# Two-layer decoder, last cross attention: two heads per instruction, score products on four row groups, and the outputs of 16 heads summed in one PSUM tile

## The chip, the core and the metric

One core of a Trainium2 chip runs one program. The metric is the device time of one execution in microseconds. The engines are TensorE (PE; its weight loads are listed as PEld), VectorE (DVE), ScalarE (ACT), GpSimd (POOL) and SyncE (SP), which issues most DMAs. They run side by side and are held in order by semaphores only.

## What is computed

Four sequences of 256 tokens with 128 channels go through two decoder layers. Only the end of layer 1 is touched by the change: its cross attention over a context of 256 tokens, followed by a mixture of experts. With 16 heads of 8 channels each, and `x` of one sequence (256 x 128), the last attention is

```
q = x @ Wq + bq;  k = ctx @ Wk + bk;  v = ctx @ Wv + bv      # each 256 x 128, 16 heads of 8
a[h] = softmax(q[h] @ k[h].T * 8 ** -0.5, axis=keys)         # 256 x 256 for each head
o[:, 8h:8h+8] = a[h] @ v[h]
x = layernorm(x + o @ Wo + bo)                               # then 8 experts, 2 of them per token
```

Everything is fp32. For the scores, q and k are split into a high and a low part, which are stacked along the contraction (3 x 8 rows for one head, 24 of a group of 32), and run as fp32r products.

## The kernel before

The five engines walk through one list of slots (`through_slots`), from slot -14 to slot 345. In a slot, each engine does its `front`, then what is due of the side jobs (`sides`: projections, the output projection and norms, the experts), then its `back`. There is no other scheduler: the order on each engine is the order of this walk. The last attention has one head per slot, from slot `LX_AT` = 235 on. Slots are counted from there in this text ("slot 10" is 235 + 10). Heads are numbered through all attentions; here n is 0 to 63 for the 4 sequences of 16 heads, four heads make a unit, four units a sequence (the code calls it a batch).

For head n, in slots:

- n: PE `head_products` multiplies queries by keys (two matmuls with 31 rows of contraction, lines 721 to 744) into the PSUM tile `SC[0]`, half n % 2; DVE `head_maximum` (L1542) takes the maximum over the 256 keys, 128x512 elements. PE may write a half again once the maximum of head n - 2 is done.
- unit start + 6 (`TURN_AT`): PE turns the maxima of the unit (`turn_shifts`, L750), ACT copies them to `shift_rows` (L1135), and SP sends them with one DMA into row 31 of each group of `packed_q` (`place_shifts`, L1804).
- n + 9 (`SHIFT_LAG`): PE `transposed_products` (L769, two matmuls, 32 rows) writes scores minus maximum, keys on partitions, into `SC[1]`, half n % 2; ACT `head_exponential` (L1169) takes the exponential, 128x512, into one of 8 buffers `exps`.
- n + 10: POOL `add_key_tiles` (L1689) adds the two key tiles of the head, 128x256, into `kept` (a part of the tile VB).
- unit start + 15 (`SUMS_AT`): PE `unit_sum` (L786) sums `kept` over keys with a matrix of ones, the unit's four heads on four column groups.
- unit start + 16 and 17: ACT copies the sums and takes exp(-ln(sum)) as a first inverse (L1162, L1163, L1175), POOL checks it (L1701), DVE refines it (L1559).
- unit start + 17 (`VALUES_AT`): PE `unit_values` (L812) multiplies values by exponentials, four heads on four column groups, into `SO`. A head has 8 channels but fills 32 rows of its group.
- unit start + 18 (`DIVIDE_AT`): DVE `divide` (L1567) writes the unit's 128x256 normalised outputs to `OB`. So there are four such tiles for a sequence.

`mix(b)` is the side job of sequence b after its last unit, from slot 16 b + 31 on (`OUT_AFTER` = 31): `project_out` (L625) at its steps 1 and 2 multiplies four 128-row chunks of `OB` by a padded Wo, for each of two token tiles; then come the norm, the router (L909, L915 to L917), and at steps 15 to 28 the experts (L923, L938, L948, L958, L969) and the last norm. The mixes of two sequences overlap with each other and with the heads of later sequences; slot 110 is the last.

Rows of a matmul decide its row group: head n sits on partitions 32 (n % 4) to 32 (n % 4) + 31 of `packed_q` and `packed_k`. In a slot the order on PE is: products of head n (front), turn, side jobs, sums and values, products of head n - 9 (back), then the products of head n + 1 in the next front.

SP's list in these slots: `place_shifts` every fourth slot, six small DMAs for each unit of the next sequences at slots 14 to 42 (`cross_in`, L1821), and the loads of the experts (`load_experts`, L1809, two of 512 KB each) at slots 8, 12, 16 and 20.

## Time and profile before

| | |
|---|---|
| time, median of 3 runs | 796.15 us (793.91 to 796.48) |
| the profiled execution | 796.1 us, of which the span in the trace is 794.3 us |
| PE busy | 719.1 us (91%), 5852 matmuls |
| PE weight loads busy | 542.2 us (68%) |
| DVE busy | 489.1 us (62%) |
| ACT busy | 412.9 us (52%) |
| POOL busy | 290.0 us (37%) |
| mean granted TensorE clock | 0.937 of full |
| first products of the last attention | 592.8 us |
| last products of the last attention | 737.4 us |

Times in the rows count from the span's start. An engine's busy time counts the instructions in flight; matmuls overlap, so a busy PE is not yet a PE at its peak. The granted clock is the share of TensorE's full 2.4 GHz: 1.00 is 2.4 GHz, 0.50 is 1.2 GHz, and a value between is a mean over a stretch with both.

### The profile page before, as it was taken

What the parts mean: (1) busy time and instruction counts of PE and PEld (TensorE: products, weight loads), DVE (VectorE), ACT (ScalarE), POOL (GpSimd) and SP (SyncE); (2) the same over time, 40 slices, a digit from 0 to 9 for tenths busy, and PEclk for the clock granted to TensorE, in tenths of its full rate; (3) what the DMA queues carried; (4) which work ended last, traced back from release to release, by engine and by line L of the source; (5) the groups of instructions that cost most, each with busy time, mean ns of one, the idle gap of its engine ahead of it and who ended that gap; (6) DMA issues with size and microseconds to landing.
All of it is one profiled execution on the core that took longest, in us unless ns stands there. A gap on an engine that the chain in (4) does not pass through costs nothing.

```text
span 794.3 us, 16402 instructions
## 1 busy us (share of the span) xinstructions
PE 719.1 (91%) x5852; PEld 542.2 (68%) x5852; DVE 489.1 (62%) x1297; ACT 412.9 (52%) x1047; POOL 290.0 (37%) x395
## 2 busy tenths in 40 slices
PE   8788889898897998999999989989888899999886
PEld 6565567575665765899898967758566455767665
DVE  4669777887977885444543455545455658583643
ACT  2234556657566677554544467555562545454311
POOL 0015355565555666110000036423350646363300
PEclk8869989999999999999999999999998756999999
DMA  8537451533727471000000000001011501000000
GB/s 235 126 69 179 123 128 43 122 83 88 161 46 205 112 214 57 2 1 1 1 1 1 1 1 4 1 2 41 4 38 54 185 26 31 2 2 9 8 7 7
DMA packets 25175, 48.11 MB, mean 61 GB/s; under 512 B 7264, under 2 KB 14192, under 8 KB 25096
## 3 DMA queue, kind: packets, MB, share of 16 engines
q1 hardware_dynamic: 24376, 45.66, 22.7%
q10 hardware_dynamic: 720, 1.41, 0.5%
q8 instruction: 48, 0.79, 0.4%
q14 instruction: 31, 0.25, 0.1%
HBM read 17.49 MB, written 0.52 MB: 23 GB/s over the span
## 4 chain that ended last, share of the span: by engine, by line
PE 60%; DVE 14%; issue 10%; ACT 8%; SPq 3%; POOL 2%; DMA 2%; POOLq 0%; ACTq 0%; DVEq 0%
PE SC L839 7%; PE G L550 7%; PE SC L826 7%; PE SC L769 5%; PE G L625 4%; PE SC L861 3%; PE G L938 3%; DVE shift_cols L1542 3%; PE SO L812 3%; ACT causal_probs L1154 2%; PE SO L893 2%; PE SC L743 2%; PE G L647 2%; SPq L1769 1%; PE G L577 1%
## 5 line engine op out<-in xcount | busy, mean ns | idle before, releaser
L1169 ACT ACTIVATE exps<-SC 128x512 f32<-128x512 f32 x192 | 114.4, 597 | 106.8 <-PE SC L769 106.1
L1542 DVE TENSOR_REDUCE shift_cols<-SC 128x2 f32<-128x512 f32 x192 | 129.5, 684 | 32.0 <-PE SC L743 31.5
L1621 POOL TENSOR_TENSOR rstd<-variance,consts 128x2 f32<-128x2 f32 (+1 forms) x48 | 36.8, 766 | 266.0 <-DVE variance L1234 263.0
L1689 POOL TENSOR_TENSOR VB<-exps 128x256 f32<-128x256 f32 x128 | 95.7, 756 | 59.4 <-ACT exps L1169 58.6
L1143 ACT ACTIVATE hidden<-SC,cols 128x256 f32<-128x256 f32 x128 | 53.6, 471 | 65.4 <-PE SC L826 65.3
L1711 POOL TENSOR_TENSOR causal_probs<-causal_probs,inverse 128x256 f32<-128x256 f32 x64 | 51.6, 828 | 68.9 <-DVE inverse L1555 68.9
L1576 DVE SCALAR_TENSOR_TENSOR R<-SC,small,R 128x128 f32<-128x128 f32 x128 | 39.0, 346 | 54.0 <-PE SC L839 53.3
L1154 ACT ACTIVATE causal_probs<-SC,negmax 128x128 f32<-128x128 f32 (+1 forms) x128 | 52.3, 424 | 37.1 <-DVE negmax L1550 37.0
L769 PE MATMUL SC<-stacked_q,stacked_k 100*128 100x256 f32 x256 | 66.9, 344 | 3.5 <-DMA stacked_q<-shift_rows 1.9
L839 PEld LDWEIGHTS SC<-ffn_w,hidden 128*128 128x128 f32 x512 | 66.0, 192 | 5.3 <-issue 1.8
L839 PE MATMUL SC<-ffn_w,hidden 128*128 128x128 f32 x512 | 67.6, 276 | 0.0
L826 PE MATMUL SC<-XN,ffn_w 128*128 128x256 f32 x256 | 66.5, 383 | 0.0
L1681 POOL TENSOR_TENSOR VB<-exps,consts 128x256 f32<-128x256 f32 x64 | 46.6, 739 | 44.8 <-ACT exps L1169 44.7
L769 PEld LDWEIGHTS SC<-stacked_q,stacked_k 100*128 100x128 f32 x256 | 40.3, 193 | 32.9 <-issue 21.9
L743 PE MATMUL SC<-stacked_k,stacked_q 96*128 96x256 f32 x256 | 56.5, 305 | 6.3 <-DVE shift_cols L1542 5.9
L1550 DVE TENSOR_REDUCE negmax<-SC 128x2 f32<-128x256 f32 x64 | 32.7, 553 | 41.2 <-PE SC L864 41.2
L1701 POOL TENSOR_TENSOR unit_sums<-unit_sums,unit_inverse 128x256 f32<-128x256 f32 x48 | 35.7, 744 | 60.8 <-ACT unit_inverse L1175 60.8
L550 PE MATMUL G<-XN,a_weights 128*128 128x256 f32 x184 | 49.2, 410 | 2.4 <-DVE Z L1320 1.5
L743 PEld LDWEIGHTS SC<-stacked_k,stacked_q 96*128 96x128 f32 x256 | 41.7, 200 | 10.8 <-DVE shift_cols L1542 9.4
L826 PEld LDWEIGHTS SC<-XN,ffn_w 128*128 128x128 f32 x256 | 44.2, 192 | 4.2 <-issue 0.8
L812 PE MATMUL SO<-exps,VB 128*32 128x256 f32 (+1 forms) x640 | 46.4, 404 | 0.0
L550 PEld LDWEIGHTS G<-XN,a_weights 128*128 128x128 f32 x184 | 35.9, 205 | 8.8 <-DVE Z L1320 1.8
(257 smaller groups left out, 1504.5 us busy)
## 6 DMA issues: line engine op xcount, KB each, us to landing
stacked_k<-k_hi SPq DMA_DIRECT2D x64, 128.0 KB, 2.4
stacked_q<-q_hi SPq DMA_DIRECT2D x64, 128.0 KB, 2.4
ffn_w<-in_ffn_w SPq DMA_DIRECT2D x16, 512.0 KB, 4.8
stacked_k<-k_lo SPq DMA_DIRECT2D x32, 128.0 KB, 2.4
stacked_q<-q_lo SPq DMA_DIRECT2D x32, 128.0 KB, 2.5
packed_k<-U SPq DMA_DIRECT2D x48, 32.0 KB, 1.9
packed_q<-YN SPq DMA_DIRECT2D x48, 32.0 KB, 1.9
a_weights<-in_a_li SPq DMA_DIRECT2D x3, 256.0 KB, 7.4
```

What stands on the lines that cost most here:

```text
L550: last = mm(g[:, k * T:(k + 1) * T], w[kr, c * P:(c + 1) * P], src[kr, :], start=True, stop=True)
L743: last = mm(SC[0][:, n % 2, t, :], q[:, t * P:(t + 1) * P], kk, start=True, stop=True)
L769: last = mm(SC[1][:, n % 2, t, :], kk[:, t * P:(t + 1) * P], q, start=True, stop=True)
L812: last = mm(g[HD * k:HD * k + HD, q0:q0 + w], v, src, start=first, stop=end)
L826: last = mm(g[:, f * T:(f + 1) * T], experts0[e // 4][0][:, at:at + P], XN[b][:, :], start=True, stop=True)
L839: last = mm(g[:, t * C:(t + 1) * C], hidden0[i % 4][:, f, t * P:(t + 1) * P], experts0[e // 4][1][:, at:at + C], start=f == 0, stop=f == 1)
L1143: last = fn(hidden0[i % 4][:, f, :], g[:, f * T:(f + 1) * T], ACT.Gelu, bias=col("ffn0_b1", 2 * e + f))
L1154: last = fn(PB[:, i % RING, k, 0:w], SC[i % 2][:, j, t, 0:w], ACT.Exp, bias=negmax[:, i % 4, k:k + 1], accum_out=sums[:, i % 4, k:k + 1])
L1169: fn(exps[:, n % EXPS, :, :].rearrange("p t q -> p (t q)"), SC[1][:, n % 2, :, :].rearrange("p t q -> p (t q)"), ACT.Exp, scale=ATTENTIONS ...
L1542: v.tensor_reduce(shift_cols[:, n // UNIT % 4, :, n % UNIT], SC[0][:, n % 2, :, :], axis=AX.X, op=ALU.max, negate=True).then_inc(head_max, 1)
L1689: v.tensor_tensor(kept[n % EXPS].rearrange("p t q -> p (t q)"), exps[:, n % EXPS, 0, :], exps[:, n % EXPS, 1, :], ALU.add).then_inc(kept_r ...
L1711: last = v.tensor_tensor(p, p, m, ALU.mult)
```

## The change

- Scores: PE works in even slots only. One block (`cross_products`) holds the products of heads n and n + 1 and the transposed ones of heads m and m + 1, with m = n - 10 (`CROSS_LAG` = 10 where it was 9), in the order n, n + 1, m, m + 1 for the first tile and then for the second: four row groups and four PSUM banks. It waits until the maxima of heads n - 2 and n - 1, and the exponentials of heads m - 2 and m - 1, are done.
- DVE (`two_maxima`), ACT (`two_exponentials`, now in `front`) and POOL (`add_key_tiles_of_two`) do two heads with one instruction.
- The value tile is spread: 32 columns for each head, zero but for its 8 channels at the place of its unit, so that the four units of a sequence add up in one 128x256 tile of `SO`. Their sums over keys do the same in the other half of `SO`, with a new constant `own_rows`. POOL clears the two value tiles once (`clear_values`); DVE writes the values in two strided instructions.
- Inverse, check, refinement and division are done once per sequence instead of once per unit, after its last values.
- `project_out` multiplies one chunk instead of four. The mix of each sequence starts one slot later (`CROSS_OUT_AFTER` = 32).

```diff
-SHIFT_LAG = 9
+SHIFT_LAG, CROSS_LAG = 9, 10
+CROSS_INVERT, CROSS_REFINE, CROSS_DIVIDE = 18, 19, 19
+CROSS_OUT_AFTER = HEADS - UNIT + CROSS_DIVIDE + 1
...
-    "lx": {"lx_wq": (C, C), "lx_wo": (P, 512)},
+    "lx": {"lx_wq": (C, C), "lx_wo": (C, C)},
...
 def project_out(s, t):
-                    if at["d"] == HD:
+                    if s // NB == LX:
+                        c0, chunks = 4 * (s % 2), 1
+                        pe.wait_ge(cross_divided, CROSS_UNIT + s % NB + 1)
+                    elif at["d"] == HD:
...
+                def cross_products(n, m):
+                    if n is not None:
...
+                        pe.wait_ge(head_max, n)
+                        if n % UNIT == 0:
+                            pe.wait_ge(packed_in[n // UNIT % 4], 16 * 6 * (stream_of(n) % NB + 1))
+                    if m is not None:
+                        pe.wait_ge(head_exp, m)
+                        if m % UNIT == 0:
+                            pe.wait_ge(shifts_in[m // UNIT % 4], 16 * (m // UNIT // 4 + 1))
+                    for t in range(TT):
+                        of = slice(t * P, (t + 1) * P)
+                        if n is not None:
+                            for h in (n, n + 1):
+                                q, kk = packed(h, HD - 1)
+                                last = mm(SC[0][:, h % 2, t, :], q[:, of], kk, start=True, stop=True)
...
+                        if m is not None:
+                            for h in (m, m + 1):
+                                q, kk = packed(h, HD)
+                                last = mm(SC[1][:, h % 2, t, :], kk[:, of], q, start=True, stop=True)
...
+                def cross_sum(U_):
+                    n, u = UNIT * U_, U_ % 4
+                    if u == 0:
+                        cross_place(stream_of(n) % NB)
+                    pe.wait_ge(kept_ready, n + UNIT)
+                    own = const("own_rows")[:, HD0 * (3 - u):HD0 * (3 - u) + HD]
+                    for k in range(UNIT):
+                        mm(SO[HD * k:HD * k + HD, T:2 * T], own, kept[(n + k) % EXPS].rearrange("p t q -> p (t q)"),
+                           start=u == 0, stop=False)
...
+                def cross_unit_values(U_):
...
+                    pe.wait_ge(head_exp, n + UNIT)
+                    for kt in range(TT):
+                        for k in range(UNIT):
+                            last = mm(SO[HD * k:HD * k + HD, 0:T], cross_value(s, kt, h0 + k), exps[:, (n + k) % EXPS, kt, :],
+                                      start=False, stop=u == 3 and kt == TT - 1)
+                    last.then_inc(cross_outputs, 1)
...
+                def cross_sums_drawn(b):
...
+                    act.wait_ge(cross_outputs, CROSS_UNIT + 4 * (b + 1))
+                    fn(unit_sums[:, b % 2, :], SO[:, T:2 * T], ACT.Copy)
+                    fn(unit_inverse[:, b % 2, :], SO[:, T:2 * T], ACT.Ln).then_inc(cross_drawn, 1)
...
+                def two_exponentials(n):
+                    unit_read(act, (n - EXPS) // UNIT)
+                    act.wait_ge(head_scores, n + 2)
+                    fn(exps[:, n % EXPS:n % EXPS + 2, :, :].rearrange("p h t q -> p (h t q)"),
+                       SC[1][:, :, :, :].rearrange("p h t q -> p (h t q)"), ACT.Exp, scale=ATTENTIONS[LX]["scale"]).then_inc(head_exp, 2)
...
+                def two_maxima(n):
+                    dve.wait_ge(shift_scores, n + 2)
+                    v.tensor_reduce(shift_cols[:, n // UNIT % 4, :, n % UNIT:n % UNIT + 2].rearrange("p t h -> p h t"), SC[0][:, :, :, :],
+                                    axis=AX.X, op=ALU.max, negate=True).then_inc(head_max, 2)
...
+                def cross_refine(b):
+                    dve.wait_ge(inverse_checked, CROSS_UNIT + b + 1)
+                    v.scalar_tensor_tensor(unit_inverse[:, b % 2, :], unit_sums[:, b % 2, :], -2.0,
+                                           unit_inverse[:, b % 2, :], op0=ALU.add, op1=ALU.mult)\
+                        .then_inc(sums_inverse, 1)
+
+                def cross_divide(b):
+                    dve.wait_ge(cross_outputs, CROSS_UNIT + 4 * (b + 1))
+                    dve.wait_ge(sums_inverse, CROSS_UNIT + b + 1)
+                    v.scalar_tensor_tensor(OB[:, 4 * (b % 2), :], SO[:, 0:T], -1.0, unit_inverse[:, b % 2, :],
+                                           op0=ALU.mult, op1=ALU.mult).then_inc(cross_divided, 1)
...
+                    k = n % EXPS
+                    both = VB[k // 4][:, 1024 + T * (k % 4):1024 + T * (k % 4 + 2)].rearrange("p (h q) -> p h q", q=T)
+                    v.tensor_tensor(both, exps[:, k:k + 2, 0, :], exps[:, k:k + 2, 1, :], ALU.add).then_inc(kept_ready, 2)
...
+                def clear_values(k):
+
+                    wait_filled(pool, ("OC", 4 * (NB - 2 + k) + 3))
+                    v.memset(VB[k][:, 0:TT * HEADS * HD], 0.0).then_inc(packed_cleared, 1)
```

## Rows read from the trace of the kernel before

**Rows 1.** Windows by stage: span, busy time of each engine (instructions), granted clock, DMA share, GB/s.
```profile
592.00:612.50 20.50, 17.47 (x128) 13.16 (x128) 10.25 (x25) 6.46 (x14) 3.05 (x4) 0.90 0.13 44
612.50:648.70 36.20, 32.71 (x221) 16.10 (x220) 21.65 (x36) 19.28 (x45) 19.28 (x27) 0.64 0.36 118
648.70:674.10 25.40, 24.39 (x186) 14.36 (x185) 20.40 (x50) 12.66 (x32) 14.96 (x20) 0.70 0.12 30
674.10:711.20 37.10, 36.13 (x358) 25.89 (x357) 25.81 (x71) 18.33 (x42) 16.48 (x23) 0.97 0.01 2
711.20:743.70 32.50, 31.41 (x308) 23.18 (x306) 17.84 (x57) 14.96 (x34) 14.88 (x21) 1.00 0.02 6
743.70:794.30 50.60, 38.95 (x340) 31.82 (x340) 22.41 (x71) 8.78 (x16) 3.83 (x5) 0.95 0.03 9
```

**Rows 2.** The same windows, only instructions on packed_q: PE, PEld, POOL busy, clock, DMA.
```profile
612.50:648.70 36.20, 15.51 (x92) 10.03 (x92) 0.00 (x0) 0.64 0.36 118
648.70:674.10 25.40, 9.30 (x58) 5.86 (x56) 0.00 (x0) 0.70 0.12 30
674.10:711.20 37.10, 8.07 (x64) 4.79 (x64) 0.00 (x0) 0.97 0.01 2
711.20:743.70 32.50, 5.49 (x24) 3.23 (x24) 0.00 (x0) 1.00 0.02 6
...
sum 202.30, PE 42.65 PEld 26.45 POOL 0.00; mean PE 7.11 PEld 4.41 POOL 0.00
```

**Rows 3.** PE timeline, one block between side jobs: start us, duration, line, operation, tiles.
```profile
688.82 0.38 PE L769 MATMUL SC<-packed_q,packed_k 32*128 32x256 f32 x1
...
689.26 2.00 PE L938 MATMUL G<-slot_tokens,ffn_w 128*128 128x64 f32 x16
```

**Rows 4.** PE timeline at 708 us: two slots' products with nothing between them.
```profile
707.95 0.38 PE L769 MATMUL SC<-packed_q,packed_k 32*128 32x256 f32 x1
707.96 0.38 PE L743 MATMUL SC<-packed_k,packed_q 31*128 31x256 f32 x1
707.97 0.38 PE L769 MATMUL SC<-packed_q,packed_k 32*128 32x256 f32 x1
707.97 0.38 PE L743 MATMUL SC<-packed_k,packed_q 31*128 31x256 f32 x1
...
708.40 1.07 PE L812 MATMUL SO<-exps,VB 128*32 128x256 f32 x16
```

**Rows 5.** Groups of instructions by line and shape, 600 to 794 us: count, busy, mean ns, idle.
```profile
L1689 POOL TENSOR_TENSOR VB<-exps 128x256 f32<-128x256 f32 x64 | 48.7, 769 | 39.5 <-ACT exps L1169 39.1
L1542 DVE TENSOR_REDUCE shift_cols<-SC 128x2 f32<-128x512 f32 x61 | 41.1, 685 | 11.4 <-PE SC L743 11.3
L1169 ACT ACTIVATE exps<-SC 128x512 f32<-128x512 f32 x64 | 38.1, 599 | 36.1 <-PE SC L769 35.6
...
L1701 POOL TENSOR_TENSOR unit_sums<-unit_sums,unit_inverse 128x256 f32<-128x256 f32 x16 | 12.2, 764 | 19.9 <-ACT unit_inverse L1175 19.9
...
L625 PE MATMUL G<-w_lx_wo,OB 128*128 128x128 f32 x64 | 10.4, 312 | 0.4 <-DVE HE L1525 0.4
...
L1162 ACT ACTIVATE unit_sums<-SM 128x256 f32<-128x256 f32 x16 | 6.1, 380 | 3.6 <-PE SM L786 3.6
```

**Rows 6.** Group of the whole span: DVE maximum over half as many elements.
```profile
L1550 DVE TENSOR_REDUCE negmax<-SC 128x2 f32<-128x256 f32 x32 | 13.6, 425 | 41.2 <-PE SC L864 41.2
```

**Rows 7.** SP's queue, timeline from 625 us: issue of shifts and of the next sequence's parts.
```profile
625.88 0.55 SPq L1804 DMA_DIRECT2D packed_q<-shift_rows  x1
626.52 1.76 SPq L1821 DMA_DIRECT2D packed_k<-U  x3
...
631.34 0.55 SPq L1804 DMA_DIRECT2D packed_q<-shift_rows  x1
```

**Rows 8.** PE timeline, the longest wait for shifts.
```profile
635.70 0.57 PE L769 MATMUL SC<-packed_q,packed_k 32*128 32x256 f32 x1 [1.52 <-DMA packed_q<-shift_rows]
```

**Rows 9.** A window of 2 us, columns as in rows 1.
```profile
642.00:644.00 2.00, 2.00 (x20) 0.81 (x19) 0.00 (x0) 0.84 (x3) 0.00 (x0) 0.50 0.07 17
```

210 lines of the change are left out of this document (143 added, 67 removed).

## Prediction

> **What bounds the kernel now.** I read the windows by stage first [rows 1]. The last attention runs from 592 us to the end, and I cut it where its side jobs change: stage A (slots 0 to 9, beside the rest of the attention before it), B (slots 10 to 33, nearly only heads, with the expert weights coming in), C (slots 33 to 46, the first sequence's norm and router), D (47 to 62, with experts of one sequence), E (63 to 78), F (the rest, no heads after slot 72). PE is busy for 36.1 of 37.1 us in D and for 31.4 of 32.5 us in E, at a clock of 0.97 and 1.00. So D and E are as long as PE's list is. In B and C PE is busy too (32.7 of 36.2, 24.4 of 25.4), but at 0.64 and 0.70: much of the list runs at 1.2 GHz, as in the window at 642 us, which has no idle time and a clock of 0.50 [rows 9]. In C, DVE is busy for 20.4 of 25.4 us and is a close second. In F PE is busy for 39 of 50.6 us, and the chain through the experts of the last sequence sets the time.
>
> Then I read what the products cost in each stage [rows 2]: 42.65 us in all, and by difference 4.3 us in A. Then what one block costs: a head's transposed products and the next head's plain ones, four matmuls on two row groups, hold PE from 688.82 to 689.26, 0.44 us [rows 3]. And where no side job stands between two slots, eight matmuls on four row groups start within 0.02 us of each other in fours, and the next job starts 0.45 us after the first [rows 4]. That is the change's block, already in the trace: eight for the price of four.
>
> **Products, PE.** After the change there are 32 even slots with a pair n and 32 with a pair m, ten slots behind: 27 blocks hold both and 5 + 5 hold one, 37 in all, of two waves each. In flight a block takes about 0.50 us at 2.4 GHz (0.44 and the tail of the last matmul), and at a clock of 0.65 to 0.70 about 0.65. A: 5 blocks, 2.5 us instead of 4.3. B: 12, 7.8 instead of 15.5. C: 7, 4.6 instead of 9.3. D: 8, 4.0 instead of 8.1. E: 5, 2.5 instead of 5.5 [rows 2]. PE saves 1.8 + 7.7 + 4.7 + 4.1 + 3.0 = 21.3 us.
>
> By the Trainium skill, page "TensorE: Matmul & The Clock Gate", section "Measured speedup vs the span model", four row tiles gave 3.07 times and not 4 times one. By that a full block would take 0.44 x 4 / 3.07 = 0.57 us and the forecast below would be 27 x 0.13 = 3.5 us later. The trace's 0.45 us for eight [rows 4] does not agree with it, and I go by the trace.
>
> **Output projection, PE.** 64 instructions and 10.4 us become 16 and 2.6 us [rows 5], saving 7.8: about 2.8 in C, where the clock is lower, and 1.6 to 1.7 in D, E and F each. Sums, values and turns keep their count and form, only with another stationary tile and other PSUM columns. So PE's list gets 29 us shorter. That is the most that can arrive.
>
> **DVE, ACT, POOL.** DVE's maximum costs 0.685 us for 512 elements and 0.425 for 256, so 1.02 ns for an element more: 1.21 us for two heads instead of 1.37 [rows 5, 6]. ACT: 0.60 for 512, 0.38 for 256, so 1.04 us instead of 1.20 [rows 5]. POOL's add of two heads lies between 0.77 and twice that [rows 5]; nothing on PE needs it before two slots later, so it is covered. Twelve of the sixteen inversions and divisions go: on POOL 12 x 0.76 = 9 us [rows 5], on DVE some 1.1 us for each, on ACT about 1.2. None of these engines is the bound outside C. The spread values cost DVE about 0.2 us for each of four sequences, POOL's two clears (1024 elements) about 1 us each in its idle time. The wider constants add 28 KB at the start: 0 to 0.3 us, I take 0.2.
>
> **The new waits.** (1) One block waits for maxima and exponentials of the pair before, and there is no second half to write into. Its round is the block, 0.5, DVE's 1.21 and two handovers, about 1.9 us for two slots. Now two slots take 3.1 us in B (36.2 / 23 slots x 2) and more elsewhere, so it is covered unless DVE comes to its maxima 1.2 us late. Queued behind PE's wait are the side jobs of both slots. (2) ACT's exponential moves from back to front, past the side jobs, and ahead of the shift copy in every second even slot; the shifts leave up to 1.04 us later and are needed one slot later. (3) SP's list is the same. With expert loads a unit takes it 5.46 us (625.88 to 631.34), without them 0.55 + 2 x 1.8, about 4.2 [rows 7]. This is a floor for B that the change leaves: B moves 5.75 units, three of them with loads, 3 x 5.4 + 2.75 x 4.2 = 28 us. To that come the wait for shifts behind the loads (1.5 us now [rows 8]) and, at slot 28, the next sequence's parts, whose tiles are free only when SP's six DMAs have landed, some 2.5 us. So B ends near 32. (4) The division comes once, after the last values of a sequence: three ACT steps of 0.4, POOL's 0.76, two DVE steps of at most 0.7 and the handovers, 3.5 us in a row [rows 5]. Between those values (slot 77 for the last sequence) and its projection (slot 81) PE has three full slots of the experts of the sequence before, 2.0 us and more each (32.5 us / 16 slots in E [rows 1]). Covered; if the cover were gone it would cost up to 3.5 us, once.
>
> **What arrives.** A: its pace is set by the older attention's softmax; 1.2 of 1.8. B: 36.2 to about 31.7, 4.5 of 7.7. C: PE's list falls to 24.4 - 4.7 - 2.8 = 16.9 us, DVE's to 20.4 - 1.1 - 2.4 = 16.9; neither packs without gaps, so about 20, saving 5.5. D: 4.1 + 1.6 = 5.7, of which 5.0, since joint waits cost a little. E: 4.6, of which 4.0. F: 1.6, of which 1.2. Sum 1.2 + 4.5 + 5.5 + 5.0 + 4.0 + 1.2 = 21.4, less 0.2 for the start: 21.2 us. The profiled execution took 796.1 us (span 794.3 and 1.8 around it), 0.05 from the median, so no correction: 796.1 - 21.2 = 774.9, say 775.
>
> **The rivals.** *The light stages keep their length* (0.16). In A to C, SP's list, the way of the shifts (maxima, turn, exponential, copy, DMA) and DVE take the place of PE, and only D, E, F arrive: 10 us, 786. For it speaks [rows 7], and that DVE is at 20.4 of 25.4 in C; against it, that PE has no idle time at 642 us at 1.2 GHz [rows 9], so that its list is the bound just there. The Trainium skill, page "TensorEngine Tiling (Array Packing)", section "PSUM Bottleneck", says that after a fourfold faster TensorE the PSUM copies may become the bottleneck; that would be this case, with the 1.9 us round as its pace.
>
> *All of PE's gain arrives* (0.16). 29 us, 767. Against: the SP floor in B. For: with four groups in a block TensorE does as much in less time; if the granted clock in B and C rises over 0.64 and 0.70, the gain there is larger than I counted, down to 763.
>
> *The four groups run one after the other* (0.05), so that the change does not do what it says: a block of eight costs 0.88, the products save nothing, and the projection and the fewer small steps leave 7 us: 789. [Rows 4] speaks against.
>
> *The clock falls in D and E* (0.04). PE less busy between joint waits could be granted 1.2 GHz for a part of it; 57 us of its list lie there after the change, and a third of it at half clock costs 19 us: 794. Against: those stages stay dense with expert matmuls, and keep 0.97 and 1.00 now with 1 us of idle time each.
>
> *One buffer is too few* (0.06), the slower side. If DVE, in order, reaches the maxima of a pair only after its side jobs, each of the 23 pairs of A to C exposes its 1.21 us and handovers, 1.4 x 23 = 32 us, against 14 us saved on PE's list there and 10 in D to F: 796 + 32 - 24 = 804. It decides once the round is longer than the 3.1 us that two slots take now.
>
> The forecast keeps 0.53, with 769 to 782 as its own range. The range that should hold 8 in 10 takes in the full gain and most of the light-stage case: 764 to 788. About 0.3%, or 2.4 us, is what a measurement can tell from no change: slower 0.06, same 0.04 (the clock case), faster 0.90.
>
> **What would show it.** The page of the changed kernel should have the same 256 product matmuls in 37 blocks of up to eight, with fours starting within 0.03 us; 16 projection instructions; DVE's maximum x32 near 1.21 us and ACT's exponential x32 near 1.04. The time from first to last products should fall from 144.5 us to about 126, D's 16 slots from 37 to about 32. The forecast is wrong if PE shows waits on the maxima or exponentials of more than 5 us in all, if waits for shifts grow over 5 us, or if a full block takes over 0.6 us at full clock.

## The result, and the profile after

The changed kernel took 800.89 us (median of 20 runs, 796.26 to 813.3) beside 794.97 us of the kernel before; the ratio is 1.0076, 95% interval 1.0054 to 1.0099. Taken again with other runs of both it was 1.0061 (1.0019 to 1.0103). So it is slower by 0.6 to 0.8%, some 6 us, where 21 us less was forecast. Medians hold all runs of a kernel, while the ratios here and below leave out its disturbed, slower runs.

The profiled execution has a span of 804.4 us. Windows by stage, which answer [rows 1]; the markers are the same jobs, the stages A to E up to the last product block at 742.3 us, then everything behind it. Columns: span, then busy time and instructions of PE, PEld, DVE, ACT and POOL, granted clock, DMA share, GB/s.

```profile
598.20:618.40 20.20, 15.98 (x128) 12.15 (x128) 10.48 (x20) 5.88 (x11) 3.21 (x4) 0.92 0.16 53
618.40:655.80 37.40, 24.94 (x217) 11.21 (x217) 17.49 (x20) 16.31 (x25) 15.70 (x14) 0.69 0.35 110
655.80:681.10 25.30, 20.02 (x181) 10.60 (x182) 18.90 (x38) 7.63 (x12) 9.39 (x8) 0.70 0.10 28
681.10:716.00 34.90, 31.61 (x346) 22.09 (x345) 24.73 (x58) 15.26 (x25) 12.60 (x12) 0.96 0.01 2
...
598.20:742.30 144.10, 115.12 (x1078) 72.39 (x1080) 85.29 (x162) 55.75 (x90) 50.65 (x45) 0.83 0.14 43
742.30:804.40 62.10, 48.48 (x410) 38.69 (x409) 27.08 (x92) 10.88 (x20) 6.22 (x7) 0.88 0.02 7
```

The kernel before, from its first to its last products and behind them, in the same columns:

```profile
592.80:737.40 144.60, 136.65 (x1132) 88.96 (x1132) 90.37 (x213) 68.88 (x157) 65.24 (x87) 0.83 0.14 43
737.40:794.30 56.90, 44.41 (x404) 35.56 (x403) 27.71 (x93) 10.80 (x22) 6.50 (x9) 0.95 0.03 8
```

That pair of lines is the case in short. From the first to the last products PE does 21.5 us less (136.65 to 115.12), and the stretch is as long as before (144.6 and 144.1): PE now waits. And the part behind the last products, in which the change only takes work away, takes 5.2 us more, at a clock of 0.88 instead of 0.95.

There may be a third part, ahead of the first products, where little but the constants and weights loaded at the start differs. The first products come at 598.2 instead of 592.8 us. In the five profiles of kernels without the tile for 16 heads, the experiments below included, they come at 588.4 to 593.7, in the mean 591.3. In the fifteen with it they come at 589.7 to 600.1, in the mean 595.0, although the time at a clock of 0.50 ahead of them is nearly the same (46 and 47 us). Most of the difference is there by 300 us already. It is larger than the scatter within the two groups leads one to expect (2 and 3 us from profile to profile), and no experiment looked for its cause. What follows is about the other two parts.

Each engine's work became what was forecast. PE's instructions on the score tiles (whole stage, compare [rows 2], 42.65 us):

```profile
sum 206.20, PE 22.55 PEld 13.95 POOL 0.00; mean PE 3.76 PEld 2.33 POOL 0.00
```

PE's timeline, one full block; the next job starts 0.44 us after the first product, where [rows 4] had 0.45:

```profile
695.37 0.38 PE L796 MATMUL SC<-packed_k,packed_q 31*128 31x256 f32 x2
695.38 0.39 PE L802 MATMUL SC<-packed_q,packed_k 32*128 32x256 f32 x2
695.60 0.28 PE L796 MATMUL SC<-packed_k,packed_q 31*128 31x256 f32 x2
695.60 0.28 PE L802 MATMUL SC<-packed_q,packed_k 32*128 32x256 f32 x2
695.81 0.37 PE L755 MATMUL G<-w_ctx_wk,CTXT 64*128 64x128 f32 x1
```

Groups from 600 us on (compare [rows 5]): busy time and mean ns behind the bar, then idle time ahead of them.

```profile
L1858 POOL TENSOR_TENSOR VB<-exps 128x512 f32<-128x512 f32 x32 | 41.4, 1295 | 44.8 <-ACT exps L1290 24.9 <-issue 19.9
L1680 DVE TENSOR_REDUCE shift_cols<-SC 128x4 f32<-128x1024 f32 x32 | 39.1, 1222 | 24.2 <-PE SC L796 24.2
L1290 ACT ACTIVATE exps<-SC 128x1024 f32<-128x1024 f32 x32 | 32.8, 1024 | 48.5 <-PE SC L802 48.4
...
L1710 DVE SCALAR_TENSOR_TENSOR unit_inverse<-unit_sums,unit_inverse 128x256 f32<-128x256 f32 x4 | 4.9, 1222 | 1.9 <-POOL unit_sums L1874 1.9
...
L662 PE MATMUL G<-w_lx_wo,OB 128*128 128x128 f32 x16 | 4.0, 332 | 5.6 <-DVE HE L1658 3.5 <-issue 2.1
```

PE's waits between first and last products: total, times, longest. First the kernel before, then the changed one.

```profile
PE SC L743 <- DVE shift_cols L1542: 3.0, 5, 1.4
...
PE SC L769 <- DMA packed_q<-shift_rows: 1.5, 1, 1.5
```

```profile
PE SC L796 <- DVE shift_cols L1680: 9.2, 8, 2.8
PE G L503 <- DVE X L1372: 5.8, 2, 3.2
PE SC L796 <- DMA packed_q<-shift_rows: 4.3, 2, 3.3
PE G L662 <- DVE HE L1658: 3.1, 2, 2.4
PE SC L796 <- ACT causal_probs L1249: 2.1, 1, 2.1
PE G L662 <- issue: 2.1, 1, 2.1
```

The maxima (L1680) and the norm of a sequence (L1372), both DVE's, lead. In all PE is idle for 29.0 us of the stretch, where it was idle for 8.0. One way in which DVE comes late shows at 663 us. DVE's timeline, POOL's, and PE's; in brackets the idle time and what ended it:

```profile
663.07 2.50 DVE L1372 TENSOR_SCALAR X<-R,moments,rstd 128x128 f32<-128x128 f32 x2 [0.82 <-POOL rstd L1778]
665.50 1.22 DVE L1680 TENSOR_REDUCE shift_cols<-SC 128x4 f32<-128x1024 f32 x1
```

```profile
663.01 2.48 POOL L1858 TENSOR_TENSOR VB<-exps 128x512 f32<-128x512 f32 x2
```

```profile
665.63 0.44 PE L503 MATMUL G<-consts,X 128*128 128x128 f32 x2 [3.19 <-DVE X L1372]
```

Two norm instructions between SBUF tiles take 2.50 us and end within 0.1 us of POOL's two long additions; PE waits 3.19 us for the norm, and the maxima come last. The kernel before has this meeting too: the same norm took 1.62 us beside two additions of 0.73 us, and those of the next two sequences, which met none, 0.59 us. DVE's timeline of the kernel before:

```profile
655.29 1.62 DVE L1244 TENSOR_SCALAR X<-R,moments,rstd 128x128 f32<-128x128 f32 x2
```

A like meeting lies in the division of three of the four sequences (a refinement takes 1.47 to 1.51 us there). POOL's timeline, then DVE's and PE's:

```profile
652.88 0.73 POOL L1874 TENSOR_TENSOR unit_sums<-unit_sums,unit_inverse 128x256 f32<-128x256 f32 x1 [5.33 <-ACT unit_inverse L1271]
653.57 1.27 POOL L1858 TENSOR_TENSOR VB<-exps 128x512 f32<-128x512 f32 x1
```

```profile
653.64 1.47 DVE L1710 SCALAR_TENSOR_TENSOR unit_inverse<-unit_sums,unit_inverse 128x256 f32<-128x256 f32 x1 [0.86 <-POOL unit_sums L1874]
```

```profile
655.75 0.76 PE L662 MATMUL G<-w_lx_wo,OB 128*128 128x128 f32 x2 [2.12 <-issue]
```

PE's 2.12 us ahead of the projection ("issue" in the profile, but the projection needs the division, which DVE does at 655.23) are the end of that chain.

### The profile page after: what moved, and what is told of

Same layout as the page of the kernel before. It is cut to its first block, busy times and chain, and to the rows that moved or that the text cites. A ratio compares the mean times of both kernels' runs of the same rounds, so it can differ in the third digit from the quotient of the medians.

```text
span 804.4 us, 16062 instructions
## 1 busy us (share of the span) xinstructions
PE 706.1 (88%) x5804; PEld 532.1 (66%) x5804; DVE 483.6 (60%) x1245; ACT 399.9 (50%) x979; POOL 276.9 (34%) x353
## 3 DMA queue, kind: packets, MB, share of 16 engines
q10 hardware_dynamic: 720, 1.44, 0.5%
## 4 chain that ended last, share of the span: by engine, by line
PE 58%; DVE 18%; issue 11%; ACT 7%; DMA 2%; POOL 2%; SPq 2%; POOLq 0%; ACTq 0%; DVEq 0%
PE G L584 7%; PE SC L923 7%; PE SC L910 7%; PE G L662 3%; PE SC L945 3%; PE SC L825 3%; PE G L1022 3%; DVE shift_cols L1675 3%; ACT causal_probs L1249 2%; PE SO L977 2%; PE SO L895 2%; PE SC L770 2%; DVE shift_cols L1680 2%; PE G L684 2%; PE G L1042 2%
## 5 line engine op out<-in xcount | busy, mean ns | idle before, releaser
L1284 ACT ACTIVATE exps<-SC 128x512 f32<-128x512 f32 x128 | 76.3, 597 | 76.5 <-PE SC L825 76.3
L1675 DVE TENSOR_REDUCE shift_cols<-SC 128x2 f32<-128x512 f32 x128 | 86.5, 683 | 19.3 <-PE SC L770 18.9
L1726 DVE SCALAR_TENSOR_TENSOR R<-SC,small,R 128x128 f32<-128x128 f32 x128 | 39.0, 346 | 54.0 <-PE SC L923 53.3
L1290 ACT ACTIVATE exps<-SC 128x1024 f32<-128x1024 f32 x32 | 32.8, 1024 | 48.5 <-PE SC L802 48.4
L1858 POOL TENSOR_TENSOR VB<-exps 128x512 f32<-128x512 f32 x32 | 41.4, 1295 | 44.8 <-ACT exps L1290 24.9
L1844 POOL TENSOR_TENSOR VB<-exps 128x256 f32<-128x256 f32 x64 | 47.6, 753 | 21.4 <-ACT exps L1284 21.1
L1680 DVE TENSOR_REDUCE shift_cols<-SC 128x4 f32<-128x1024 f32 x32 | 39.1, 1222 | 24.2 <-PE SC L796 24.2
L584 PE MATMUL G<-XN,a_weights 128*128 128x256 f32 x184 | 50.6, 419 | 2.6 <-DVE Z L1448 1.5
```

The lines of the kernel that those rows point to most:

```text
L584: last = mm(g[:, k * T:(k + 1) * T], w[kr, c * P:(c + 1) * P], src[kr, :], start=True, stop=True)
L1284: fn(exps[:, n % EXPS, :, :].rearrange("p t q -> p (t q)"), SC[1][:, n % 2, :, :].rearrange("p t q -> p (t q)"), ACT.Exp).then_inc(head_ex ...
L1675: v.tensor_reduce(shift_cols[:, n // UNIT % 4, :, n % UNIT], SC[0][:, n % 2, :, :], axis=AX.X, op=ALU.max, negate=True).then_inc(head_max, 1)
L1680: v.tensor_reduce(shift_cols[:, n // UNIT % 4, :, n % UNIT:n % UNIT + 2].rearrange("p t h -> p h t"), SC[0][:, :, :, :], axis=AX.X, op=ALU ...
L1844: v.tensor_tensor(kept[n % EXPS].rearrange("p t q -> p (t q)"), exps[:, n % EXPS, 0, :], exps[:, n % EXPS, 1, :], ALU.add).then_inc(kept_r ...
```

## The experiments

Theory 1: the joint waits of a pair hold PE. Theory 2: DVE's queue is held, by the division once per sequence and by POOL's long additions. Theory 3: the granted clock takes part of the time. Theory 4: the shifts' DMAs come late, behind expert loads. The table has every kernel that was run; "ratio" is against the kernel before in the same rounds, the rest is from each kernel's one profile: length from first to last products and behind them, and in brackets the us of it at a clock of 0.50.

| kernel | median, us | ratio (95%) | first to last | behind |
|---|---|---|---|---|
| before | 794.97 | 1 | 144.5 (48) | 56.9 (5) |
| before_again | 794.97 | one run | 146.1 (51) | 56.9 (5) |
| changed | 800.89 | 1.0076 (1.0054 to 1.0099) | 144.2 (48) | 62.1 (15) |
| changed_again | 800.02 | 1.0061 (1.0019 to 1.0103) | 145.3 (58) | 60.5 (11) |
| pair_only | 801.04 | 1.0088 (1.0056 to 1.0119) | 144.0 (41) | 57.1 (1) |
| pair_adds | 794.37 | 1.0007 (0.9974 to 1.0040) | 140.2 (38) | 58.1 (6) |
| pair_adds_loads | 798.15 | 1.0051 (1.0022 to 1.0080) | 144.6 (58) | 61.7 (15) |
| tile_only | 796.18 | 1.0013 (0.9989 to 1.0037) | 139.7 (48) | 71.0 (38) |
| tile_loads | 800.56 | 1.0101 (1.0028 to 1.0174) | 140.5 (44) | 61.6 (14) |
| no_refine | 796.07 | 0.9987 (0.9948 to 1.0025) | 141.2 (51) | 59.6 (8) |
| single_adds | 797.55 | 1.0010 (0.9977 to 1.0043) | 136.4 (38) | 65.8 (26) |
| adds_loads | 796.48 | 1.0042 (1.0012 to 1.0073) | 135.8 (38) | 62.1 (15) |
| adds_loads_divide | 796.69 | 0.9994 (0.9959 to 1.0028) | 138.3 (48) | 72.8 (42) |
| split_waits | 797.30 | 1.0030 (1.0000 to 1.0061) | 138.9 (48) | 62.1 (15) |
| half_maxima | 794.70 | 0.9934 (0.9898 to 0.9969) | 136.5 (51) | 63.7 (19) |
| short_adds | 791.62 | 0.9944 (0.9917 to 0.9972) | 132.3 (41) | 62.2 (15) |
| filled | 805.72 | 1.0133 (1.0076 to 1.0191) | 150.0 (51) | 56.7 (2) |
| last_filled | 794.14 | 0.9998 (0.9971 to 1.0024) | 138.2 (41) | 61.8 (15) |
| best_filled | 793.38 | 0.9967 (0.9927 to 1.0007) | 137.5 (41) | 61.7 (15) |
| no_refine_adds_loads | 790.83 | 0.9940 (0.9905 to 0.9975) | 135.3 (38) | 59.5 (9) |

Verdicts go by the ratios. The last two columns are one execution each, and not always a typical one: the profiled run of pair_only took 794.3 us, where the median is 801.0, and that of tile_only 805.5, where it is 796.2. So the profile of pair_only can't show where its 7 us lie. Two kernels leave out arithmetic that the result needs, half_maxima and short_adds, and three leave out the step that corrects the inverse: no_refine, best_filled and no_refine_adds_loads.

**The two halves of the change.** The pairing alone, on the kernel before:

```diff
-head_products(n) ... transposed_products(n - 9)
+cross_products(n, m)      # heads n, n + 1, m, m + 1 in one block, m = n - 10
+two_maxima, two_exponentials, add_key_tiles_of_two
```

> The kernel before with the pairing alone: two heads share one maximum, one exponential and one addition, and the products go in blocks of four rows' groups; sums, values, division and the projection in four pieces stay as before, unit by unit. Theory 1 (the joint waits of a pair, on one buffer, hold PE): the time stands with the changed kernel or above it, 798 to 806 us, and PE waits some 20 us for the maxima and exponentials of a pair. Theory 2 (the division once per sequence holds DVE's queue and PE): the product blocks' gain stays and the time falls to 780 to 790 us, since the long division chain isn't there. Theory 3 (the granted clock falls because of gaps on PE): the clock of the stretches in which PE waits is at 0.50 as in the changed kernel, and a gain, if any, is under 5 us.

And the rest alone, one head per slot as before:

```diff
-SHIFT_LAG, CROSS_LAG = 9, 10
+SHIFT_LAG, CROSS_LAG = 9, 9
-cross_products(n, m), two_maxima, two_exponentials, add_key_tiles_of_two
+one head each, in front and back; 16 heads in one tile and one division per sequence stay
```

> The changed kernel with one head per slot as in the kernel before (its own maximum, exponential, addition, products spread in front of and behind the round), but with the outputs of 16 heads in one tile, one division per sequence and a projection in one piece. Theory 1 (the pairs' waits are the loss): the projection's and divisions' gain stays, the time is 785 to 792 us, against 795 before. Theory 2 (the division once per sequence is the loss): the time is 798 to 806 us, with PE waiting 1.5 to 2.5 us ahead of each of the four projections. Theory 3: no opinion on the sign, but the clock would follow PE's gaps.

The pairing alone costs what the whole change costs, 1.0088; the tile of 16 heads alone is level, 1.0013. Theory 2, as stated for these two, falls: the division per sequence is not the main loss, the pairing is. But neither range that was set for the tile alone was met (785 to 792 us, or 798 to 806). In its profile the stretch from first to last products is 4.8 us shorter than before, with PE idle for only 10.9 us, and the part behind is 14 us longer, with 38 us at 0.50 (in the profile of tile_loads 4.7 us longer, with 14). So the tile's gain arrives between the products and is gone from the whole.

In pair_only, PE's sums (L814) also wait for POOL's additions themselves:

```profile
PE SM L814 <- POOL VB L1750: 6.1, 4, 1.7
```

The changed kernel shows no such wait of PE, but for 0.2 us of one weight load.

**POOL's long addition,** in the changed kernel and in pair_only:

```diff
-v.tensor_tensor(both, exps[:, k:k + 2, 0, :], exps[:, k:k + 2, 1, :], ALU.add).then_inc(kept_ready, 2)
+for h in range(2):
+    v.tensor_tensor(both[:, h, :], exps[:, k + h, 0, :], exps[:, k + h, 1, :], ALU.add).then_inc(kept_ready, 1)
```

> The changed kernel with POOL's one addition of 128x512 per pair of heads issued as two of 128x256. Nothing is left out. Part of theory 2 (DVE's operations between SBUF tiles stand while POOL's 1.3 us addition runs): DVE's norm, refinement and index operations come back to their durations of before (the norm's 444 ns instead of 732 ns), and the time falls by 2 to 5 us, to 796 to 799 us. Theory 1: POOL's second dispatch costs and nothing is gained, 800 to 803 us.

> The kernel before with the pairing alone, as in the kernel of that name, and POOL's addition of a pair issued as two of 128x256. Nothing is left out. If POOL's long addition costs the pairing as much as it costs the changed kernel (801 against 797.5 us there), the time falls from 801 to 797 or 798 us, and DVE's maxima stand between products 3 us less. Rival: with sums and divisions by the unit the long addition did no harm, and the time stays at 800 to 802. In both cases, with the projection in four pieces, the clock behind the last products should stay at 1.00 but for 1 to 6 us.

> The changed kernel once more. If the long additions are the cause, the products from first to last take 143 to 146 us again, DVE's refinement and norm stand at 1.2 us and 0.7 us or more on average, and the time is 4 to 8 us over the kernel before. If the difference was only from run to run, this profile may have the stage at 136 to 141 us.

The shorter additions take POOL longer in all (64 of 765 ns, busy for 47.6 us instead of 41.4), and the kernels are faster: 1.0076 becomes 1.0010, and on the pairing alone 1.0088 becomes 1.0007, with intervals apart in both. From first to last products the changed kernel takes 144.2 and 145.3 us in its two profiles and 136.4 with split additions. Windows of single_adds, columns as above:

```profile
594.80:731.20 136.40, 110.35 (x1080) 69.52 (x1080) 79.69 (x162) 55.75 (x90) 56.63 (x76) 0.86 0.14 45
731.20:797.00 65.80, 53.05 (x410) 44.27 (x408) 27.19 (x92) 10.98 (x20) 6.36 (x8) 0.80 0.02 7
```

DVE is busy 5.6 us less with the same instructions. Not all of the 8 us between the first and the last products is this: the clock was at 0.50 for 38 us instead of 48. The size is rough. With the repeats (1.0076 and 1.0061 against 1.0010 and 1.0042; for the pairing 1.0088 against 1.0007 and 1.0051) the intervals overlap, single differences run from 1.5 to 6.4 us, and their means are 3 and 5 us. One experiment goes further and nearly takes the additions away (it leaves out most of the sums):

```diff
+to = slice(0, T if n < STACK_HEADS + EXPS else 16)
-v.tensor_tensor(both[:, h, :], exps[:, k + h, 0, :], ...)
+v.tensor_tensor(both[:, h, to], exps[:, k + h, 0, to], ...)
```

> The changed kernel with small additions, of which those from the ninth head of the stage on add only the first 16 of 256 columns. Left out: the rest of these sums. POOL's busy time in the stage falls by some 25 us. If what is left of POOL's additions still holds DVE up, DVE's operations between SBUF tiles take what they take alone (the refinement 0.42 us instead of 0.7, the norm 0.44 instead of 0.68), the stage falls from 136.4 to under 134 us, and the time by 2 to 4 us from 797.5. If the split of the additions had already given all, both stay within 1.5 us.

The same two norm instructions, DVE's timeline of single_adds and then of short_adds; the changed kernel's took 2.50 us:

```profile
657.75 1.44 DVE L1372 TENSOR_SCALAR X<-R,moments,rstd 128x128 f32<-128x128 f32 x2 [0.82 <-POOL rstd L1778]
```

```profile
659.00 0.60 DVE L1372 TENSOR_SCALAR X<-R,moments,rstd 128x128 f32<-128x128 f32 x2 [0.82 <-POOL rstd L1778]
```

2.50, 1.44, 0.60 us: the time of a DVE operation between SBUF tiles follows the length of the POOL operation beside it. The maxima, which read PSUM, keep 1222 ns in all of them. The norm had not come back to its duration of before with split additions, as was expected (on average 680 ns; 471 before, 810 in the changed kernel); with short ones it did (470). The stage falls on to 132.3 us and the ratio to 0.9944, whose interval lies clear below those of both measurements of the changed kernel. That settles that the additions cost time. It does not settle that they do it through the maxima. PE's waits for these are as long as ever in the changed kernel (9.2 us), in single_adds (8.5) and in short_adds:

```profile
PE SC L796 <- DVE shift_cols L1680: 9.3, 11, 2.5
```

What falls from one to the next of the three is PE's wait for the norms (5.8, 4.7, 3.9 us) and ahead of the projections (6.1, 4.3, 3.1). With the pairing alone, the waits for maxima do fall, from 6.5 to 3.2 us, while the sums' waits for POOL grow from 6.1 to 7.0. The Trainium skill, page "SBUF — State Buffer", section "Who interferes with whom", says that DVE and GpSimd share one pair of ports under an exclusive lock, and that a DVE instruction which needs that pair, or POOL's, waits for the whole instruction of the other. The three times of the norm agree.

**Joint waits and the length of the maxima.**

```diff
+# transposed products of m, m + 1: wait for exponentials and shifts only, four matmuls
+# then products of n, n + 1: wait for maxima only, four matmuls
```

> The changed kernel with small additions, and with the eight products of a pair's block issued as two blocks of four in two groups of rows: first the transposed ones, which wait for the exponentials and the shifts alone, then those for the maxima, which wait for the maxima alone. Nothing is left out. PE then has about 0.44 us more of products in each of the 28 to 32 double blocks, some 13 us of busy time. Theory 1 in its narrow form (it is the joint wait that delays the exponentials): the time falls by 2 to 5 us from 797.5 us in spite of it, since the transposed products no longer wait for DVE. Rival (the pair's products themselves aren't the limit and the waits stand for a queue of DVE that is late anyway): the time stays within 2 us, PE's waits fall by just the 13 us that its busy time grows. Third: the time rises by over 5 us, the cheap products were worth that.

> The changed kernel with small additions, and DVE's maximum of a pair over half of the columns. Left out: the other half of each maximum, so the shifts aren't the true maxima; the same instructions otherwise. If the length of DVE's maxima (1.22 us) is what PE's 16.4 us of waits for them stand for, the maximum takes about 0.69 us, 32 x 0.53 = 17 us of DVE go, the products from first to last take 126 to 130 us instead of 136.4, and the time falls by 5 to 8 us from 797.5. If the waits stand for DVE's queue being held by other engines (norms, divisions, POOL, ACT), the stage stays over 133 us and the time falls by 0 to 3 us.

```diff
-v.tensor_reduce(shift_cols[...], SC[0][:, :, :, :], ...)
+v.tensor_reduce(shift_cols[...], SC[0][:, :, :, 0:P], ...)
```

Both have the split additions. With separate waits the time is the same within the intervals (1.0030 and 1.0010): PE is busy for 118.2 us instead of 110.4, and idle for 20.7 instead of 26.0. PE's waits for maxima fall from 8.5 us to 1.6, with 3.0 us for exponentials in their place. So the joint wait does hold PE, and what its parting gives back is spent on products that no longer share a block. The experiment doesn't tell what the joint wait alone costs: theory 1 is neither shown nor refuted, only that parting the waits in this way gains nothing. Halved maxima leave out half of the scores, so that the shifts are not the true maxima. They take 0.69 us, DVE's busy time falls from 79.7 to 64.8 us, and the ratio is 0.9934, outside the interval of single_adds. PE's waits for maxima fall:

```profile
PE SC L796 <- DVE shift_cols L1680: 4.1, 5, 2.0
```

from 8.5 us in 9 waits. The profile's first to last products stay at 136.5, but with 51 us at 0.50 instead of 38. So the length of the maxima counts too, by a part that the clock blurs.

**The division.** Without the refinement, and one slot later:

```diff
-dve.wait_ge(sums_inverse, ...); OB = SO * -1.0 * refined inverse
+dve.wait_ge(first_inverse, ...); OB = SO * 1.0 * exp(-ln(sums))
```

```diff
-CROSS_INVERT, CROSS_REFINE, CROSS_DIVIDE = 18, 19, 19
+CROSS_INVERT, CROSS_REFINE, CROSS_DIVIDE = 18, 20, 20
```

> The changed kernel without POOL's check product and DVE's refinement of the inverse: the division multiplies by the exponential of minus the logarithm alone. Left out is the one correcting step of the inverse of the sums, four times in all; nothing else. Theory 2 (division chain): in the changed kernel DVE's refinement takes 1.2 us on average and waits for POOL before it, some 2 to 2.5 us per sequence ahead of the projection or the norm; the time falls by 4 to 8 us, to 793 to 797 us. Theory 1 (pairs' waits): it falls by 0 to 2 us, since PE waits on the maxima all the same.

> As the kernel with small additions and later loads, and DVE's refinement and division of a sequence one slot later (20 instead of 19 behind), the projection with them. Nothing is left out. Theory 2 (DVE's queue stands behind the refinement, which waits for ACT's guess and POOL's check): 2 to 4 us less than the kernel without this edit, PE's waits for maxima fall by that. Rival: the projection and the norm that wait for the division come a slot later, and for the last sequence that is on the path: 0 to 2 us more.

No refinement, and with it no check product on POOL: 0.9987 beside 1.0076, so this part of the division chain is worth some 7 us by the two ratios (6 against the repeat, whose interval it touches), and what 2 us for each of four sequences would make; 3.0 us of it show from first to last products (141.2). Theory 2 may be back in this form: not the division once per sequence as such (tile_only has it too), but the chain in DVE's queue together with pairs that wait for DVE. That it takes both is argued: PE's waits for maxima stay at 9.0 us without the refinement, and those ahead of the projection fall from 6.1 to 2.8. One slot later is inconclusive: 0.9994 beside 1.0042, intervals that don't part, and in its one profile the 90 us at 0.50 hide all else.

**Later loads.** Three kernels test this edit, and four more of the table carry it (adds_loads_divide, last_filled, best_filled, no_refine_adds_loads):

```diff
-if slot == LX_AT + 8 + 4 * g:     # load_experts
+if slot == LX_AT + 11 + 4 * g:
```

> The changed kernel with POOL's additions of 128x256 and the last experts' loads three slots later in SP's order (slots 11, 15, 19 and 23 of the stage instead of 8, 12, 16 and 20), so that the copies of the shifts don't stand behind two loads of 512 KB. Nothing is left out. Theory 4 (the shifts' DMAs behind the loads are a term of their own): PE's two waits for shifts, 4.3 us together in the changed kernel and 4.4 with the small additions, go, and the time falls by 3 to 4 us against 797.5 us of the small additions alone, to 794. Rival: the next wait (DVE's maxima, 16.4 us ahead of weight loads and 8.5 us ahead of products) takes it up and the time stays within 1.5 us of 797.5. Granted clock: span against mean clock should lie on the same line as the other kernels', with 0.3 to 0.4 us for each us at 1.2 GHz.

> One head per slot, one tile for 16 heads, one division per sequence, and the last experts' loads three slots later in SP's order. Nothing is left out. Theory 4: the two waits for shifts (3.8 us, the longest 3.6) go, and the time falls from 796.2 us by 3 us, to 793, which would beat the kernel before by 2 us. Rival: with PE busy in 129 of 140 us of the stage the loads only come into another DMA's way (the packed copies of the next sequence), no change within 1.5 us.

> The kernel before with the pairing alone, small additions, and the last experts' loads three slots later. Nothing is left out. The pairing with small additions took 794.4 us beside 795.5 of before. If the shifts' DMAs behind the loads are a term, 1 to 3 us less than that: 791.5 to 793.5, and faster than the kernel before by over 0.3%. If not, 794 to 795.5.

In adds_loads the edit did not do what it should. SP's queue:

```profile
630.75 1.01 SPq L1994 DMA_DIRECT2D ffn_w<-in_ffn_w  x2
631.80 0.54 SPq L1989 DMA_DIRECT2D packed_q<-shift_rows  x1
```

The two loads stand right ahead of a shift again, as in the changed kernel (636.70 and 637.76 us), and PE's waits for shifts stay at 3.9 us (4.4 in single_adds). In tile_loads they did fall, from 3.8 us in tile_only to 1.3, and the time did not (1.0013 and 1.0101, this one with 5 runs only). The other two pairs are in effect repeats, and show how far one differs: pair_adds 1.0007 and 1.0051, single_adds 1.0010 and 1.0042. So nothing here shows a gain from earlier shifts, and what the 4.3 us of waits for them cost in the changed kernel is open.

**The clock.** In the changed kernel the projection behind the last products is two matmuls where there were eight. PE's timeline of the changed kernel, and of the kernel before:

```profile
755.55 0.46 PE L662 MATMUL G<-w_lx_wo,OB 128*128 128x128 f32 x2 [0.43 <-DVE HE L1658]
756.61 2.00 PE L1022 MATMUL G<-slot_tokens,ffn_w 128*128 128x64 f32 x16 [0.60 <-ACT weight_by_slot L1101]
758.45 0.55 PE L662 MATMUL G<-w_lx_wo,OB 128*128 128x128 f32 x2
759.48 1.09 PE L1032 MATMUL G<-consts,weight_of_slot 128*128 128x128 f32 x4 [0.49 <-DVE HE L1658]
```

```profile
749.30 1.13 PE L625 MATMUL G<-w_lx_wo,OB 128*128 128x128 f32 x8 [0.43 <-DVE HE L1525]
750.36 2.00 PE L938 MATMUL G<-slot_tokens,ffn_w 128*128 128x64 f32 x16
752.20 1.11 PE L625 MATMUL G<-w_lx_wo,OB 128*128 128x128 f32 x8
```

What the projection gave up became gaps, and then the clock is at half (window of the changed kernel, columns as above).

```profile
759.00:769.00 10.00, 9.52 (x58) 8.26 (x58) 3.03 (x11) 2.21 (x4) 0.71 (x1) 0.51 0.01 2
```

The table's profiles bear this out. In 11 of the 12 in which each half of the last projection is two matmuls, the clock is at 0.50 for a while between the last products and PE's next long wait, which comes 30 to 43 us after them. Of the 8 in which it is eight matmuls, one has such a stretch, for 3.4 us. The projection was then filled up again with matmuls that repeat the first and add nothing:

```diff
+for again in range(4):      # filled: every sequence; last_filled: the last one alone
     last = mm(g[:, 0:C], OB[...], W[...], start=..., stop=...)
```

> The changed kernel, with each of the two matmuls of a projection issued four times onto the same piece, each time from the start, so that the result is the same and PE has the eight matmuls of the kernel before to do there. Nothing is left out, 24 matmuls that bring nothing are added, 0.8 us of PE at full clock per half of a projection, 6.6 us in all. Theory 3 (in the last sequences the projection was what filled PE between two waits; with it at a quarter, PE's gaps around 755 to 759 us bring the granted clock to 0.50 for ten us, twice the time for everything until 769): the time falls by 2 to 4 us in spite of the added work, to 797 to 799 us, and the stretch behind the last product block has under 6 us at 0.50. Rival (the clock falls by itself, from run to run): the time stays or rises by 1 to 5 us, and the clock there is as low as in the changed kernel.

> The changed kernel with small additions and later loads, and with the projection's matmuls four times each for the last sequence alone (6 matmuls more that bring nothing). Nothing is left out. Theory 3: behind the last product block the clock is at 0.50 for 1 to 6 us instead of 15, that part takes 57 us instead of 62.1, the stage stays at 136 us, and the time falls from 796.5 us by 2 to 4 us, to 793 or 794. Rival: the clock falls there anyway a little later, 795.5 to 797.5 us.

> The kernel before once more, for a second profile: how much of the granted clock changes from run to run. Theory 3: behind the last products the clock is at 0.50 for 1 to 8 us again, whatever it is ahead of the stage. Rival: 10 us or more there, as in the changed kernel.

With all projections filled the part behind takes 56.7 us with 2 us at 0.50, as before the change, but the added matmuls (48 instructions in the trace) cost 5.8 us ahead of it (150.0), where they stand on the path: 1.0133, with an interval that overlaps that of the changed kernel. With the last alone filled the clock holds until 768, and then it falls for 14 us behind the next wait of 2.04 us, one that the kernel before has too:

```profile
768.00:782.00 14.00, 13.29 (x60) 10.39 (x58) 2.78 (x6) 2.83 (x5) 0.00 (x0) 0.52 0.04 11
```

So the gap moved, and the gain with it; 0.9998 beside 1.0042 of adds_loads has intervals that overlap. Over all twenty profiles the part behind the last products is 55.9 us + 0.40 us for each us at 0.50 (a straight line through them, none off by over 1.1 us). By that line, 4 of the changed kernel's 5.2 us there are the clock, and the rest is within its scatter.

**Both terms together.**

> The changed kernel with small additions, later loads, no refinement of the inverse (left out: the correcting step of the inverse of the sums, four times) and the projection's matmuls four times each. If the terms add up (small additions 3.4 us, refinement 3 to 5 us, filled projection 2 to 4 us), 788 to 791 us, which beats the kernel before by 4 to 6 us. If the waits take the place of one another, 793 to 796 us.

> The changed kernel with small additions, later loads and without the refinement of the inverse (left out: the correcting step, four times); no matmuls added. The kernel with all of this and the projection's matmuls four times each had a stage of 137.5 us and 793.4 us; without the added ones the stage is 132 to 134 us and the time 788 to 791 us, 4 to 7 us under the kernel before. Rival: the granted clock behind the stage takes it back, 793 to 795 us with 15 to 40 us at 0.50 behind the last product block.

The first came to 0.9967, 793.4 us: by its expectation that is where the terms don't add up. Its added matmuls are on the path, as in filled. The second, split additions, later loads and no refinement with no matmuls added, has 0.9940 (0.9905 to 0.9975), 790.8 us beside 795.7; the two terms alone would make 1.0076 - 0.0066 - 0.0089 = 0.992. Both do less arithmetic than the kernel before, the correcting step of the inverse, so that the gain is not one at equal work. The windows of the second:

```profile
591.40:726.70 135.30, 111.55 (x1080) 70.41 (x1080) 78.44 (x159) 55.72 (x90) 54.92 (x73) 0.86 0.14 45
726.70:786.20 59.50, 45.75 (x410) 36.08 (x408) 26.25 (x91) 10.88 (x20) 5.46 (x7) 0.93 0.03 8
```

PE is still idle for 23.8 us of 135.3.

## Why the prediction was wrong

**Products and projection on PE: right.** Forecast 21.3 and 7.8 us; measured 42.65 - 22.55 = 20.1 and 10.4 - 4.0 = 6.4. A full block takes 0.44 us: eight matmuls on four groups take what four on two take [rows 3]. The Trainium skill's 3.07 times (page "TensorE: Matmul & The Clock Gate", section "Measured speedup vs the span model") is for four groups against one, at 512 columns. No run here has one group alone at these 256 columns, but the 0.57 us that the prediction made of it did not come.

**DVE's and ACT's durations: right.** 1.22 and 1.02 us, forecast 1.21 and 1.04.

**The failed step: that other engines' work is covered, so that nearly all of PE's saving arrives.** From first to last products PE's list got 21.5 us shorter, and its idle time went from 8.0 to 29.0 us. Three terms were called covered and put at nothing, POOL's addition, the new joint wait and the division; 21.4 of the 29 us were taken to arrive, and the clock behind the last products was taken to stay as it was.

**POOL's addition.** It was bounded at 0.77 to 1.54 and "covered", since nothing on PE needs it soon. Its 1.295 us lie in the bounds; that nobody waits for its result is true of the changed kernel. Its cost came another way: it holds up DVE's norm (471 ns before, 810 now), refinement (691 and 1222) and the like. The price, 3 to 5 us by the means of the split additions, has no place in a sum that asks only who reads the result.

**The new waits.** (1) "Covered unless DVE comes to its maxima 1.2 us late": it does, at 13 places if the weight loads' waits are counted, up to 3.1 us. This is the rival "one buffer is too few" in kind, at 9 us of PE's waits (17 by the weight loads) instead of the 32 that it was given. I gave it 0.06. It is also over the 5 us that were set as a sign of a wrong forecast. (4) The division's 3.5 us in a row was put beside PE's slots for the last sequence; but it also stands in DVE's queue for each sequence, and refinement plus long additions made it longer. I asked who needs the division, not what waits behind it on DVE.

**What arrives: wrong in A to C, half right in D, wrong in E.** A and B together: 55.9 us before, 57.6 after, and between 53.3 and 62.1 in every version tried. One unit took 6.2 us there (shifts issued at 612.91 and, five units on, at 644.15), and 5.9 before. My 5.4 took SP's busy time for the round's length, which also has maxima, turn, copy and DMA in it; in B PE waits 6.7 us for maxima and 4.3 for shifts. That this round is a floor is argued, since no run shortened it alone. C 25.3 instead of 20. With split additions it was 23.9, with halved maxima besides 21.6 at nearly the same clock (0.69 and 0.70), and with short additions 20.0, at a clock of 0.84. So DVE was the bound, for a large part at least, as it was a close second in [rows 1] at 20.4 of 25.4; it was busy for 18.9 of the 25.3, three quarters. D 34.9 instead of about 32. E (716.0 to 750.0) 34.0 and in the second profile 32.5, where 28.5 was forecast and 32.5 was before. That is the rival "the light stages keep their length", and its 786 was short by what D, E and F also lost.

**F: wrong.** 1.2 us less was forecast; it took 54.4 us instead of 50.6 [rows 1], with the clock at half for 15 us instead of 5. Over the runs, time at 1.2 GHz is twice (1 - mean clock) times the span: 113 us in the 20 runs of the changed kernel, 99 in 34 of the kernel before, and a straight line through either kernel's runs rises by 0.30 us for each. By that line some 4 of the 6 us go with the clock; it is a comparison of runs, not an experiment. The rival "the clock falls in D and E" had the right kind and the wrong place. That the removed projection work is what lets the clock fall is shown at its own place only (filled, last_filled, and the count over the table); why a stretch at half clock behind the same 2.04 us wait lasts 3 us in one run and 14 in another is open.

**What stays open.** The terms of this section are not a sum that closes: additions, refinement, maxima and clock were each measured in other company and overlap. The cost of the joint wait alone, that of late shifts, and the 4 us by which the first products come later with the new tile have no experiment.

## What to carry to other kernels

When PE's list gets shorter, ask of each other engine what stands in its queue ahead of the instruction that PE will wait for next: DVE was busy for 85 of 144 us, in order, and PE still waited for it. Keep POOL's elementwise work in short instructions while DVE works between SBUF tiles; merging two into one saved POOL 6 us here and cost the kernel some 3 to 5. Count work removed from PE in a thin stretch at less than its price, since the clock may take it back, as behind the last products here. And look at more than one profile of each kernel before calling a difference chance.

## What the hardware showed that was not expected

- Two DVE operations of 128x128 between SBUF tiles took 2.50, 1.44 and 0.60 us beside POOL additions of 512, 256 and 16 columns (1295, 765 and 260 ns).
- Kernels that are alike but for what they load at the start come to the same point at 588.4 to 600.1 us, with 41 to 58 us at 0.50. One profile there says little; five against fifteen differ by 4 us in the mean.
- Behind one wait of PE of 1.6 to 2.05 us, which all twenty profiles have, the clock was at half for 3.4 us in nine of them and for 13.7 in six; in four it did not fall there, and in one it was at half already.
